# Global attention: the product with the values moved to the middle of a key tile and one key tile later

## The reference

```python
q = _rope(q)
k = _rope(k)
scale = 1.0 / jnp.sqrt(jnp.asarray(Dh, dtype=x.dtype))
scores = jnp.einsum('blhd,bmhd->bhlm', q, k) * scale
attn = jax.nn.softmax(scores, axis=-1)
out = jnp.einsum('bhlm,bmhd->blhd', attn, v).reshape(B, L, D)
```

## Time and profile before

| | before |
|---|---|
| median of 3 runs | 2490.89 us (2490.42 to 2492.18) |
| the profiled execution | 2489.49 us, span 2487.7 us |
| PE / PEld busy | 2340.7 / 1412.1 us |
| DVE / ACT / POOL busy | 1625.5 / 1420.7 / 616.3 us |
| products with the values (L591) | first at 191.0 us, last at 884.1 us of the span |
| mean granted TensorE clock | 0.975 of full speed |

### The profile page before, as it was taken

The page is one execution under the profiler, slowest core; times in us unless marked ns, Lnnn a source line. Parts: engine busy times, 40 slices in busy tenths (PEclk is TensorE's granted clock), DMA queues, the critical chain, the costliest instruction groups (busy, mean ns, idle before and its releaser), DMA issues. The chain is left out here.

```text
span 2487.7 us, 40290 instructions
## 1 busy us (share of the span) xinstructions
PE 2340.7 (94%) x12576; PEld 1412.1 (57%) x12576; DVE 1625.5 (65%) x3713; ACT 1420.7 (57%) x2634; POOL 616.3 (25%) x484
## 2 busy tenths in 40 slices
PE   7969999999999979899999999999899999999968
PEld 4533333333333357667667667667667667667534
DVE  5778999999999746646646556546645646646326
ACT  2207777777777756547557556457456547557321
POOL 4412100000000044333323323323234233323000
PEclk9969999999999989999999999999999999999989
DMA  4583212111221010000000000000000000000006
GB/s 151 186 245 111 61 52 60 50 46 57 60 60 52 14 41 1 1 1 1 0 0 0 0 0 25 1 9 22 13 1 1 0 0 0 0 0 0 0 21 196
DMA packets 71891, 95.83 MB, mean 39 GB/s; under 512 B 13884, under 2 KB 49168, under 8 KB 71696
## 3 DMA queue, kind: packets, MB, share of 16 engines
q1 hardware_dynamic: 71808, 94.78, 12.5%
HBM read 60.67 MB, written 39.49 MB: 40 GB/s over the span
## 5 line engine op out<-in xcount | busy, mean ns | idle before, releaser
L655 DVE TENSOR_REDUCE maxima<-ps_m 128x1 f32<-128x512 f32 x1024 | 635.1, 684 | 64.0 <-PE ps_m L546 60.0
L718 ACT ACTIVATE probs<-ps_st 128x1024 f32<-128x1024 f32 x512 | 496.1, 1021 | 173.3 <-PE ps_st L578 171.8
L546 PE MATMUL ps_m<-k_st,q_st 48*128 48x512 f32 x1024 | 391.0, 468 | 31.8 <-DMA k_st<-ks 15.8
L578 PE MATMUL ps_st<-q_st,k_st 50*128 50x512 f32 x1024 | 306.7, 426 | 2.9 <-DMA q_st<-max_rows 1.8
L1236 ACT ACTIVATE l_probs<-l_probs,l_neg_max 128x256 f32<-128x256 f32 x512 | 253.5, 496 | 71.6 <-DVE l_neg_max L1365 69.2
L578 PEld LDWEIGHTS ps_st<-q_st,k_st 50*128 50x128 f32 x1024 | 160.6, 186 | 223.9 <-ACT probs L718 190.5
L591 PE MATMUL ps_o<-probs,v_st 128*32 128x512 f32 x2048 | 274.5, 608 | 0.6 <-ACT probs L718 0.6
L1215 ACT COPY p_turned<-ring 128x512 f32<-128x512 f32 x256 | 144.3, 592 | 227.4 <-PE ring L1030 227.4
L546 PEld LDWEIGHTS ps_m<-k_st,q_st 48*128 48x128 f32 x1024 | 172.0, 190 | 148.2 <-DVE maxima L655 125.8
L1365 DVE CUSTOM_DVE_ANT_1 l_probs<-ring,l_mask 128x256 f32<-128x256 f32 x384 | 145.4, 422 | 130.2 <-PE ring L1067 124.2
L990 POOL TENSOR_SCALAR clipped<-sumsq 128x16 f32<-128x16 f32 x64 | 16.2, 253 | 807.1 <-DVE sumsq L1342 807.1
(11 more groups left out here) (152 smaller groups left out, 3980.9 us busy)
## 6 DMA issues: line engine op xcount, KB each, us to landing
qs<-split SPq DMA_DIRECT2D x16, 512.0 KB, 3.5
ks<-split SPq DMA_DIRECT2D x16, 512.0 KB, 5.1
q_st<-qs SPq DMA_DIRECT2D x64, 128.0 KB, 2.6
k_st<-ks SPq DMA_DIRECT2D x64, 128.0 KB, 3.2
o<-o_sb SPq DMA_DIRECT2D x32, 256.0 KB, 2.4
x_in<-in_L_attn_x_dram SPq DMA_DIRECT2D x8, 512.0 KB, 6.3
v<-v_sb SPq DMA_DIRECT2D x16, 256.0 KB, 4.7
q_st<-qs SPq DMA_DIRECT2D x64, 64.0 KB, 2.9
```

What stands on the lines that cost most here:

```text
L546: nc.tensor.matmul(bank(base, use)[:, :], q_st[u][r, qt * P:(qt + 1) * P], k_st[u][r, h * CH:(h + 1) * CH], start=True, stop=True).then_in ...
L578: mm = nc.tensor.matmul(ps_st[j][:, h * CH:(h + 1) * CH], k_st[u][r, kt * P:(kt + 1) * P], q_st[u][r, h * CH:(h + 1) * CH], start=True, st ...
L655: nc.vector.tensor_reduce(maxima[:, par, side(e), tile + e // 4, e % 2:e % 2 + 1], bank(base, k + e)[:, :], AX_X, ALU.max).then_inc(m_used, 1)
L718: nc.scalar.activation(probs[:, kt % 4, j, :], ps_st[j][:, :], ACT.Exp, scale=float(G_DIM) ** -0.5).then_inc(exp_done, 1)
```

## The change

The product of a key tile is issued between the scores of the two heads instead of behind both, and is that of two key tiles before instead of one (`LAG` = 2). A key tile becomes: S00 m0, S01 m1, product of kt - 2, S10 m2, S11 m3. At key tile 6: transposition, m0, m1, product of key tile 4, S00, S01, S10 m2, S11 m3. The products of key tiles 6 and 7 come in key tiles 0 and 1 of the next unit. ACT's copy of `ps_o` moves behind the exponentials of key tile 1. The wait for `v_placed` moves into `product`. No instruction of computation is added or removed.

```diff
@@ -385,6 +385,7 @@
+        LAG = 2
@@ -580,8 +581,10 @@
-                def product(n, kt, u):
-
+                def product(n, kt, i, u):
+
+                    if u == 0:
+                        pe.wait_ge(v_placed, TILES * i + kt + 1)
                     pe.wait_ge(exp_done, 2 * TILES * n + 2 * kt + 2)
@@ -591,6 +594,15 @@
+                def late_product(i, n, kt, u, first):
+
+                    if kt >= LAG:
+                        product(n, kt - LAG, i, u)
+                    elif u:
+                        product(n - 1, TILES + kt - LAG, i, u - 1)
+                    elif not first:
+                        product(n - 1, TILES + kt - LAG, i - 1, NB - 1)
@@ -612,29 +624,26 @@
-                            for j in range(2):
+                            if kt == TURN:
+                                for e in (0, 1):
+                                    if m:
+                                        maxima_scores(base, *m[e])
+                                late_product(i, n, kt, u, first)
                                 for h in range(2):
-                                    e = 2 * j + h
-                                    if kt == TURN and j == 0:
-                                        if m and h == 0:
-                                            maxima_scores(base, *m[0])
-                                            maxima_scores(base, *m[1])
-                                        scores(n, kt, u, j, h, more1)
-                                    else:
-                                        scores(n, kt, u, j, h, more1)
-                                        if m:
-                                            maxima_scores(base, *m[e])
-                            if u == (1 if kt == 0 else 0):
-
-                                pe.wait_ge(v_placed, TILES * i + (kt - 1) % TILES + 1)
-                            if kt:
-                                product(n, kt - 1, u)
-                            elif u:
-                                product(n - 1, TILES - 1, u - 1)
-                            elif not first:
-                                product(n - 1, TILES - 1, NB - 1)
+                                    scores(n, kt, u, 0, h, more1)
+                            else:
+                                for h in range(2):
+                                    scores(n, kt, u, 0, h, more1)
+                                    if m:
+                                        maxima_scores(base, *m[h])
+                                late_product(i, n, kt, u, first)
+                            for h in range(2):
+                                scores(n, kt, u, 1, h, more1)
+                                if m:
+                                    maxima_scores(base, *m[2 + h])
                         if last and u == NB - 1:
-                            product(n, TILES - 1, u)
+                            for kt in range(TILES - LAG, TILES):
+                                product(n, kt, i, u)
@@ -719,7 +728,7 @@
-                            if kt == 0:
+                            if kt == LAG - 1:
                                 if u:
                                     copy_o(n - 1, i, u - 1)
```

## The result

| | before | after |
|---|---|---|
| median | 2490.65 us (4 runs) | 2549.93 us (4 runs, 2548.36 to 2553.18) |
| ratio, 95% interval | | 1.0241 (1.0223 to 1.0258) |
| the profiled execution | 2489.49 us, span 2487.7 us | 2548.36 us, span 2546.6 us |
| DVE busy / idle before its maxima reductions | 1625.5 / 64.0 us | 1629.5 / 116.4 us |

The change costs 59.3 us, 2.4%. The forecast was 2539, with a range of 2517 to 2557: sign and range held, the size came out 11 us short. First the page of the kernel after: busy time and idle time of the groups that the change touches.

What follows compares the result with a forecast made beforehand. A loop through the three banks (2.71 us per key tile) was taken to bound the kernel. 28.8 for the copy's wait plus 19.2 at key tile 6 gave 48.0 us more, hence 2539 us, range 2517 to 2557.

Steps and rivals of the forecast that it cites:

- The pace: Plain key tile: a loop of DVE, m3, product, next first pair and DVE again sets the pitch at 2.71 us.
- Rival A: Plain key tiles: the banks don't bound them, each gains 0.26 and the kernel gets faster, 2481 us; chance 5%.
- So 0 for each of the 240-odd plain tiles: Plain key tiles: the loop stays at 2.71 with other numbers on the maxima, so no gain or loss.
- The copy's wait: Product of key tile 0 waits 0.93 us for ACT's copy of the sums, in 31 units: 28.8 us.
- 0.14 after its shown end: Key tile 1: ACT's copy of the sums starts 0.14 us after the second exponential ends.
- Key tile 6: S00 and S01 alone behind the product delay what follows; 0.64 us net of the old 0.21, in 30 units: 19.2 us.
- The transposition is hidden: Key tile 6: it fits under m1's wait for DVE with 0.06 us to spare, saving the old 0.21.
- rival D: Key tile 6: the transposition isn't hidden, 0.54 us more in 31 units, 17 us, so 2556 us; chance 7%.
- B: Key tile 6 costs nothing new, only the wait for ACT's copy remains: 2520 us; chance 10%.
- C: Product of key tile 0: its wait for ACT's copy is covered, leaving 19.2 us: 2510 us; chance 4%.
- both new waits: Product of key tile 0 waiting for ACT's copy, 28.8 us, and the delays at key tile 6, 19.2 us.
- The rule weighed: Transposition's borders: changing tiling mode drains the engine; two more borders a unit, taken as hidden; if paid, 2556 us.

Runs made afterwards that it cites:

- old_bank_shift: The kernel before, with the places of the maxima in the three banks shifted by two uses: 2507.06 us (ratio 1.0068).
- bank_shift: The changed kernel, with the places of the maxima in the three banks shifted by two uses: 2536.45 us (ratio to before 1.0186).
- turn_twice: The changed kernel, with the transposition issued twice into the same place: 2549.52 us.
- the move alone: The changed kernel with LAG 1 instead of 2, so the product sits mid-tile but is that of the key tile before: 2603.27 us (1.0459).

## Why the prediction came out as it did

**The pace was read right.** The loop through three banks and the product gives 2.71 wherever the product stands between two maxima. After the change the plain pitch is 2.71 to the hundredth, though the trace still puts a wait of 0.84 on the exponentials there (530.47), as in the earlier trace rows. Rival A is out: PE's waits for ACT in plain key tiles were names, not causes.

**"So 0 for each of the 240-odd plain tiles" is the step that failed.** It rests on "there are three banks", that is, on a turn of three uses, which is false for two of the 32 uses of a unit; the lines that say so are in `before` and `place`. In the old order these two uses stood away from the product, so the trace showed no cost; the change put one of them ahead of it. That is 30 x 0.60 = 18.0 us (the last unit has no maxima), shown by adding and by removing it.

**The copy's wait: right mechanism, too large.** Taken 0.93, measured 0.69, 31 x 0.69 = 21.4 instead of 28.8. The step at fault is the gap behind the exponential. I took 0.14 after its shown end, from the earlier trace rows, so 1.16 after its start; after the change the copy starts 0.92 after the exponential's start (525.12 to 526.04), as a second exponential would. The rest of the chain held within 0.06. The 0.14 wasn't a gap behind the exponential at all, but the copy's wait for the product of key tile 7, which in the old order comes late (519.88 - 518.67 = 1.21). With the banks shifted in the old order that product is held up by 0.60 against the exponentials, and the copy goes with the product:

```profile
518.67 1.06 PE L591 MATMUL ps_o<-probs,v_st 128*32 128x512 f32 x8
...
527.96 0.59 ACT L708 COPY o_sb<-ps_o 128x512 f32<-128x512 f32 x1 [0.66 <-PE ps_o L591]
```

The first line is of the kernel before; the second, of old_bank_shift, stands 1.21 behind its product (526.75), but some 1.67 behind the exponential's start, where it was 1.16. In the new order the product is long done and only the exponential is in front.

**Key tile 6: right mechanism, somewhat too small.** Taken 0.85 over the plain pitch, measured 0.95 in the 24 units of the loop and 0.79 in units 0 to 3, 28 and 29. The 0.16 between them is made of an exponential that starts 0.51 instead of 0.43 behind S01 and an m0 that starts 0.08 instead of 0.01 behind S00 (540.53 to 540.61), each behind a wait that had just been released. In the loop such waits compare with values held in registers, outside it with constants; that this is the reason is argued, not shown. The transposition is hidden as forecast, and by more than the 0.06 that the forecast gave it, so rival D is out, and B and C as well, since both new waits appear at their places.

**The account.** The first product moved from 191.0 to 191.5, the last from 884.1 to 947.6: the stage grew by 62.9. Units 1 to 29 give 24 x 2.03 + 5 x 1.87 = 58.1 of it: 17.4 by the short turn, 20.0 by the copy, 20.7 by key tile 6. Unit 0 grew by 0.7, unit 30 by 2.5 and the last by 1.4. Some 3.4 of these is clock: in this one execution it was granted at half from 921.5 to 925 and from 931.7 to 938.5, and bank_shift, at 1.00 there, takes 34.7 for the last two units instead of 38.2. The span grew by 58.9, since what comes behind the last product took 1599.0 instead of 1603.6. That part is the same code in all kernels and lay between 1598.8 and 1606.9 in the eleven profiled executions, which also limits what a comparison of two medians can say here: pitches in the timeline are sharper.

My sum was 48: 7.4 too much at the copy, 2.0 too little at key tile 6 (24 x 0.74 + 6 x 0.58 = 21.2 in my 30 units), 18.0 missing. That the time lies in the range is in part luck: with the short turn added the forecast would have been 2557, the upper end, which was drawn for rival D; without the 7.4 at the copy and the 4.6 behind the last product, which have nothing to do with it, the time would have been 2562.

**The rule weighed.** The border ahead of the transposition costs what the earlier trace rows suggested (0.33, from 536.23 to 536.56), and this border and the one behind it are covered. The Trainium skill, TensorEngine Tiling (Array Packing), section Key Properties, has the engine drained at each change of tiling mode. The trace is in line with it: in turn_twice the second transposition, with no change between, starts 0.12 after the first, and the next maxima start 0.20 after it. But the weight loads differ as well (0.09 and 0.18), so the price of a change alone isn't shown; whatever it is, here it is hidden.

## What to carry to other kernels

When an order with a resource loop in it is rearranged, write down for each buffered instruction which earlier use it waits for, with the wrap-around of the ring where the count doesn't divide: an irregular turn cost nothing here until the expensive instruction was put behind it. Moving the long product among the instructions that wait for buffers didn't change the pace of the loop (2.71 in both orders), and the edges of the unit (opening a sum, a shared corner of PSUM) then decided. A releaser named for a wait is to be checked against its own end: 0.94 us before the waiting instruction, it released nothing. The same holds for a gap behind an instruction: the 0.14 between exponential and copy belonged to another wait, that for the product.

## What the runs showed that I had not expected

- **Matmuls on different rows overtake each other.** In key tile 6 the program has S10, m2, S11, m3 behind S00 and S01. The record of the four scores after the change begins at 538.60 and is 0.73 long; with 0.39 for the last of them, the last two, S01 and S11, began at 538.94. So S11 began 0.24 ahead of m2 at 539.18, which stands before it in the program. m2 uses the rows of S00 and S01, S11 the other ones. By these starts, a matmul on free rows didn't stand behind one on busy rows. The Trainium skill, TensorE: Matmul & The Clock Gate, Part 3, has matmuls start and end in program order; this trace disagrees for two row groups.
- **The half clock can come in the middle of the stage.** With the move alone it stood at 0.51 from 308 to 328 us and at 0.50 in the whole last unit, where PE waited 1.11 us at each product. The profiled execution of the kernel after has single products of 1.93 in its last unit too, the kernel before none; bank_shift, with the same order of products, has none either, so this differs between executions or with small shifts.
